# Attention scores from two fp32r parts on half the array's rows, in place of three bf16 parts on half its columns

## What is computed

```python
x = x + 0.5 * ffn(layernorm(x))
h = layernorm(x)                                  # (16, 256, 256)
q, k, v = (heads(h @ W.T) for W in (Wq, Wk, Wv))  # 16 heads of 16
q, k = rope(q), rope(k)
s = where(causal, q @ k.T / 4, -inf)              # (16, 16, 256, 256)
x = x + merge(softmax(s) @ v) @ Wo.T
x = x + 0.5 * ffn(layernorm(x))
```

## Time and profile before

| what | us |
|---|---|
| runs | 603.33 median, 602.26 to 603.72 |
| profiled execution, span from first to last instruction | 600.8 |
| median less that span | 2.5 |
| PE / PEld busy | 567.2 / 496.4 |
| DVE / ACT / POOL busy | 458.9 / 345.2 / 229.3 |

### The profile page before, as it was taken

The page is one execution under the profiler, slowest core; times in us unless marked ns, Lnnn a source line. Parts: engine busy times, 40 slices in busy tenths (PEclk is TensorE's granted clock), DMA queues, the critical chain, the costliest instruction groups (busy, mean ns, idle before and its releaser), DMA issues.

```text
span 600.8 us, 17866 instructions
## 1 busy us (share of the span) xinstructions
PE 567.2 (94%) x6596; PEld 496.4 (83%) x6596; DVE 458.9 (76%) x928; ACT 345.2 (57%) x610; POOL 229.3 (38%) x446
## 2 busy tenths in 40 slices
PE   1999999999789999999999999999888999999998
PEld 1789999999668888888888888888665788999997
DVE  5977777779797978879788788877562777777765
ACT  2765454546246666776667766567545655455453
POOL 6383333332665354444544445434141033333310
PEclk9999999999999999999999999999989999999999
DMA  6530000000987567654576546765400011111111
GB/s 221 199 112 6 0 0 0 0 0 1 257 219 207 167 164 208 172 157 146 166 204 177 158 139 175 197 186 159 138 2 3 1 36 35 35 35 35 35 35 36
DMA packets 71190, 63.45 MB, mean 106 GB/s; under 512 B 4178, under 2 KB 64370, under 8 KB 71154
## 3 DMA queue, kind: packets, MB, share of 16 engines
q1 hardware_dynamic: 69970, 62.81, 36.1%
q10 hardware_dynamic: 1184, 0.14, 0.2%
HBM read 33.03 MB, written 29.36 MB: 104 GB/s over the span
## 4 chain that ended last, share of the span: by engine, by line
PE 82%; DVE 10%; DMA 3%; ACT 2%; issue 1%; POOL 1%; SPq 1%; ACTq 0%; DVEq 0%
PE bank L173 18%; PE bank L537 18%; PE bank L1065 13%; PE bank L673 6%; PE bank L1060 6%; PE bank L1121 5%; PE bank L1196 4%; PE bank L1161 3%; PE bank L156 2%; PE bank L1124 2%; PE bank L1134 2%; DVE mx L863 2%; DVE g_lo L257 2%; PE bank L1184 1%; DMA w1f<-w1t 1%
## 5 line engine op out<-in xcount | busy, mean ns | idle before, releaser
L863 DVE TENSOR_REDUCE mx<-bank 128x2 f32<-128x512 f32 (+1 forms) x192 | 118.7, 684 | 31.3 <-PE bank L1065 31.2
L240 ACT ACTIVATE g<-bank,b1c 128x512 f32<-128x512 f32 x128 | 88.0, 690 | 65.6 <-PE bank L173 62.5
L537 PE MATMUL bank<-w2q,g_hi 128*128 128x256 f32 x512 | 124.4, 284 | 1.3 <-DVE g_lo L257 0.9
L537 PE MATMUL bank<-w2q,g_lo 128*128 128x256 f32 x512 | 122.5, 280 | 0.0
L985 ACT ACTIVATE probs<-bank 128x512 f32<-128x512 f32 x192 | 111.2, 597 | 11.9 <-PE bank L1065 4.4
L537 PEld LDWEIGHTS bank<-w2q,g_hi 128*128 128x128 f32 x512 | 96.5, 188 | 2.9 <-DVE w2q L375 1.1
L537 PEld LDWEIGHTS bank<-w2q,g_lo 128*128 128x128 f32 x512 | 96.5, 188 | 0.6
L315 POOL TENSOR_TENSOR res<-res,b2h 128x1024 f32 (+1 forms) x16 | 38.3, 2394 | 133.0 <-DVE xn L147 128.9
L257 DVE TENSOR_TENSOR g_lo<-g,g_hi 128x512 fp32r<-128x512 f32 x128 | 82.8, 689 | 3.1
L173 PE MATMUL bank<-xt_hi,w1q 128*128 128x512 f32 x240 | 77.3, 404 | 2.0 <-DVE xt_lo L167 2.0
L173 PE MATMUL bank<-xt_lo,w1q 128*128 128x512 f32 x240 | 76.4, 400 | 0.0
(11 more groups left out here) (129 smaller groups left out, 1170.1 us busy)
## 6 DMA issues: line engine op xcount, KB each, us to landing
qk_slots<-parts SPq DMA_DIRECT2D x32, 384.0 KB, 3.6
q<-qk_slots SPq DMA_DIRECT2D x32, 384.0 KB, 4.0
k<-qk_slots SPq DMA_DIRECT2D x32, 384.0 KB, 4.5
qk_slots<-parts SPq DMA_DIRECT2D x32, 256.0 KB, 3.4
res<-x SPq DMA_DIRECT2D x8, 512.0 KB, 3.6
qk_slots<-parts SPq DMA_DIRECT2D x32, 128.0 KB, 3.2
out<-res SPq DMA_DIRECT2D x7, 512.0 KB, 2.9
w1f<-w1t SPq DMA_DIRECT2D x2, 512.0 KB, 6.1
```

Of the source, the lines that this page charges most:

```text
L240: nc.scalar.activation(g[:, f, :], of[:], ACT.Gelu, bias=b1c[:, f:f + 1]).then_inc(g_ready, 1)
L537: last = nc.tensor.matmul(to[:, 0:D], part[:, f, t * P:(t + 1) * P], w2q[:, f, :], start=f == 0 and part is g_hi, stop=f == FC - 1 and par ...
L863: nc.vector.tensor_reduce(o, i, AX.X, ALU.max).then_inc(s_done, 1)
```

## The change

q and k become two fp32r parts (top and low): three products of parts, 48 rows, with 3 fence rows and 2 of the maxima 53, which fit into half the array's rows. Even batches live in partitions 0 to 63, odd ones in 64 to 127 of one tile each for q and k. `units` issues a straight product of batch p+1 and a turned one of batch p by turns, on the two row halves, over all 128 output columns; the two fence products come last, with an identity, or one with its halves swapped where input and output halves differ. The middle part, its rest on VectorE and its cast on ScalarE go (also in the turning at the end of the first feed-forward stage); the stores are four per batch, of the same bytes. xn is made by GpSimd, in two ops over two row tiles. The maxima are two fp32r parts, transposed as fp32 into a projection bank; those of half 1 are now transposed in the period after (MT(p, 1) is of batch p). att_t is allocated outside the stage and first holds the constant rows; a swapped identity is made by GpSimd in the first feed-forward stage (a memset and two selects). The period is laid out in four groups, in all engines' lists: on VectorE maxima 0, rope 0, normed 0, maxima 1, rope 1, statistics, maxima 2, normed 1, low_att, maxima 3, low_xt, add_output; on ScalarE exponentials 0, copy_heads 0, copy_max 1, exponentials 1, top 0, copy_max 0, exponentials 2, copy_heads 1, copy_v, copy_att, exponentials 3, copy_xt, top 1. In the last period ScalarE does both gelus' work ahead of copy_att. Cut to its core:

```diff
-PARTS = 3
-SLOTS = 6
+PARTS = 2
+SLOTS = 3
...
-Q_RUNS = ((0, 0, 2), (2, 0, 3), (5, 0, 1))
-K_RUNS = ((0, 0, 3), (3, 0, 1), (4, 0, 2))
+Q_RUNS = ((0, 0, 1), (1, 0, 2))
+K_RUNS = ((0, 0, 2), (2, 0, 1))
...
-        q6, k6 = zip(*([sb(f"{n}6_{p}", [ROWS, HEADS, SEQ], BF16) for n in "qk"] for p in range(2)))
+        q_rows, k_rows = (sb(f"{n}_rows", [P, HEADS, SEQ], F32R) for n in "qk")
...
+        def rows(of, par, first, end):
+            return of[HALF_ARRAY * par + first:HALF_ARRAY * par + end]
...
+                par = p.parity(1 - h)
+                sp.wait_ge(mt_sb, 2 * (p.p + 1 - h) + h + 1)
+                sp.dma_start(rows(q_rows, par, SCORED, ROWS)[:, HALF * h:HALF * h + HALF, :].bitcast(F32), mt[h][:].bitcast(F32))\
+                  .then_inc(m_loaded[par][h], 16)
...
+            def step(p):
+                if p.has(0):
+                    max_rows(p, 1)
                 if p.has(2):
-                    load(p, h)
-                if h == 1 and p.has(3):
+                    load(p, 0)
+                if p.has(3):
                     store(p, 0, Q_RUNS)
+                if p.has(1):
+                    max_rows(p, 0)
+                if p.has(2):
+                    load(p, 1)
+                if p.has(3):
...
+                pool.tensor_tensor(m_parts[:, :, 0, :].bitcast(F32R), mx[:, h, :, :], zero[:], ALU.add).then_inc(max_s, 1)
+                pool.wait_ge(max_s, 2 * n + 1)
+                pool.tensor_tensor(m_parts[:, :, 1, :].bitcast(F32R), mx[:, h, :, :], m_parts[:, :, 0, :], ALU.subtract)\
+                    .then_inc(max_s, 1)
...
+                pool.wait_ge(top_s, 2 * b + t + 1)
+                pool.tensor_tensor(parts[par][:, t, 1, :], rot[:, t, :], parts[par][:, t, 0, :].bitcast(F32), ALU.subtract)\
+                    .then_inc(low_s, 1)
...
+            def normalise(p):
+                b, par = p.p + 4, p.parity(4)
+                pool.wait_ge(rstd_s, 2 * p.turn(4))
+                if p.has(2, 2):
+                    pool.wait_ge(xt_lo_s, b - 3)
+                own = slice(QT * par, QT * par + QT)
+                pool.tensor_tensor(xn[:, own, :], res[:, bass.ts(b, QT), :], mean[:, own].unsqueeze(2).broadcast_to([P, QT, D]),
+                                   ALU.subtract).then_inc(xn_s, 1)
+                pool.wait_ge(xn_s, 2 * b - 3)
+                pool.tensor_tensor(xn[:, own, :], xn[:, own, :], rstd[:, own].unsqueeze(2).broadcast_to([P, QT, D]),
+                                   ALU.mult).then_inc(xn_s, 1)
+            def step(p):
...
+                if opening:
+                    normals(p)
+                if p.has(1):
+                    pad(p)
...
+                if p.has(3):
+                    rotate(p, 0)
+                if p.has(1):
+                    split_max(p, 0)
+                if p.has(3):
+                    low(p, 0)
+                    rotate(p, 1)
+                if p.has(4, 2):
+                    normalise(p)
+                if p.has(3):
+                    low(p, 1)
+                if p.has(1):
+                    split_max(p, 1)
+                if p.par == 1 and p.has(5, 2, BATCH - 2) and not opening:
+                    normals(p)
...
+            def exponentials(p, g):
+                for u, at in enumerate((4 * SEQ, 0, 2 * SEQ)):
+                    n = 3 * g + u
+                    if n % 6 == 0 and (p.has(-1) or g):
+                        act.wait_ge(pv_done, 2 * p.p + g // 2)
                     act.wait_ge(t_ready, UNITS * p.p + n + 1)
...
+            def fence(to, mask, par, half):
+                own = slice(HALF_ARRAY * par, HALF_ARRAY * par + HALF_ARRAY)
+                return nc.tensor.matmul(to[:, :, bass.ts(half, HALF_ARRAY)], (ident_b if half == par else ident_swap)[own, :],
+                                        mask[own, own].unsqueeze(1).broadcast_to([HALF_ARRAY, to.shape[1], HALF_ARRAY]), start=False, stop=half == 1, skip_group_check=True)
+            def score(to, weights, moving, first):
+                nc.tensor.matmul(to, weights, moving, start=first, stop=False, skip_group_check=True)
+            def units(p, n):
+                g, u = n // 3, n % 3
+                straight, turned_too = p.has(1), p.has(0)
+                if straight:
+                    b, par = p.p + 1, p.parity(1)
+                    if n == 0 and not p.has(-1):
+                        pe.wait_ge(swap_ready, 3)
+                        pe.wait_ge(rows_in[par], 48)
+                        pe.wait_ge(y_done, CT * CHUNKS + 2)
+                    if n % 6 == 0:
+                        pe.wait_ge(loaded[par][n // 6], LOADS * (p.turn(1) + 1))
+                    if p.has(0) or n >= 3:
+                        pe.wait_ge(s_done, UNITS * b + n - 2)
+                    s, s_par = s_ring[u], par
+                    q, k = rows(q_rows, par, 0, SCORED), rows(k_rows, par, 0, SCORED)
+                if turned_too:
+                    if n % 6 == 0:
+                        pe.wait_ge(m_loaded[p.par][n // 6], 16 * (p.turn(0) + 1))
+                    if p.has(-1) or n >= 2:
+                        pe.wait_ge(t_done, UNITS * p.p + n - 1)
+                    t, t_par = t_ring[n % 2], p.par
+                    tq, tk = rows(q_rows, t_par, 0, ROWS), rows(k_rows, t_par, 0, ROWS)
                 if u == 0:
-                    fence(r[:].rearrange("p (a k) -> p a k", a=4), mask_qk[:, 0:4, :])
                     for j in range(4):
-                        h = 4 * g + j
-                        last = halves(r[:, j * P:(j + 1) * P], q[0:SCORED, h, 0:P], k[0:SCORED, h, 0:P], j == 3)
+                        h, at = 4 * g + j, slice(j * P, (j + 1) * P)
+                        if straight:
+                            score(s[:, at], q[:, h, 0:P], k[:, h, 0:P], j == 0)
+                        if turned_too:
+                            score(t[:, at], tk[:, h, P:SEQ], tq[:, h, P:SEQ], j == 0)
                 else:
-                    fence(r[:].rearrange("p (a k) -> p a k", a=2)[:, :, P:SEQ], mask_qk[:, 0:2, :])
                     for j in range(2):
-                        h = 4 * g + 2 * u - 2 + j
-                        last = halves(r[:, j * SEQ:(j + 1) * SEQ], q[0:SCORED, h, P:SEQ], k[0:SCORED, h, :], j == 1)
...
+                        h, at = 4 * g + 2 * u - 2 + j, slice(j * SEQ, (j + 1) * SEQ)
+                        if straight:
+                            score(s[:, at], q[:, h, P:SEQ], k[:, h, :], j == 0)
+                        if turned_too:
+                            score(t[:, at], tk[:, h, 0:P], tq[:, h, :], j == 0)
+                for half in range(HALVES):
+                    if straight:
+                        to = s[:].rearrange("p (a k) -> p a k", a=4) if u == 0 else s[:].rearrange("p (a k) -> p a k", a=2)[:, :, P:SEQ]
+                        s_last = fence(to, mask_qk, s_par, half)
+                    if turned_too:
+                        to = t[:].rearrange("p (a q) -> p a q", a=4) if u == 0 else t[:].rearrange("p (a q) -> p a q", a=2)[:, :, 0:P]
+                        t_last = fence(to, mask_kq, t_par, half)
+                if straight:
+                    s_last.then_inc(s_ready, 1)
+                if turned_too:
+                    t_last.then_inc(t_ready, 1)
+            def group(p, g):
+                for n in range(3 * g, 3 * g + 3):
+                    units(p, n)
...
+                pe.wait_ge(max_s, 2 * (2 * (p.p + 1 - h) + h) + 2)
+                if h == 0:
+                    if p.has(3):
+                        pe.wait_ge(rope_s, 2 * (p.p + 3) + 1)
+                    elif p.has(-2):
+                        pe.wait_ge(att_lo_s, p.p - 1)
+                elif p.has(-2):
+                    pe.wait_ge(wo_done, p.p)
+                else:
+                    pe.wait_ge(v_done, p.p + 3)
                 for t in range(QT):
-                    last = nc.tensor.transpose(mt_bank[:, t * P // 2:(t + 1) * P // 2].bitcast(BF16),
...
+                group(p, 0)
...
+                if p.has(3):
+                    QK(p, 0)
+                if p.has(0):
+                    MT(p, 1)
+                if p.has(-1):
+                    OT(p, 0)
+                group(p, 1)
...
+                if p.has(3):
+                    QK(p, 1)
+                if p.has(0):
+                    PV(p, 0)
                 if p.has(1):
-                    MT(p, h)
+                    MT(p, 0)
+                group(p, 2)
...
+                if p.has(3):
+                    V(p)
+                if p.has(-1):
+                    ANT(p)
                 if p.has(0):
-                    PV(p, h)
+                    OT(p, 1)
+                group(p, 3)
+                if p.has(4, 2):
+                    XT(p)
...
+                if p.has(-1):
+                    WO(p)
...
+                if p.has(0):
+                    PV(p, 1)
```

463 lines of the change are left out of this document (172 added, 291 removed).

## The result

The changed kernel takes **641.0 us** (median of 4 runs, 637.72 to 641.99) against 603.13 (602.26 to 603.72) in the same session: ratio 1.0611, interval 1.0591 to 1.063. The forecast was 617 with a range up to 638: right in sign, about 24 us short. The profiled execution's span is 638.7 us against 600.8, so 37.9 us are to be found.

What follows compares the result with a forecast made beforehand. TensorE's program of a period was taken as the bound: +1.0 us a period gave +13, the start +2.4, the last two periods -1.5, so 13.9 on a 600.8 us span; forecast 617 us, range 594 to 638.

Steps and rivals of the forecast that it cites:

- What bounds the kernel: In an attention period, TensorE's own program sets the length, 18.76 us; the change was priced as its new length.
- the two-bank wait: In each group, the third step waits for the first exponential to free its turned bank: half a microsecond.
- C: In scoring, loads on the two row halves queue for one path: 2.55 us a group, 646 us; chance 0.10.
- A: In scoring, loads cost 0.055 us and tiling overheads hide: groups of 1.73 us, 596 us; chance 0.16.
- B: In scoring, row halves give all they can: 1.1 us a group, 570 us; chance 0.06.
- the exit: On TensorE, the time from the last score pairs to the transposes behind them, 0.10 us each.
- A group's length: In scoring, three steps take 2.00 us with the wait, four groups 8.0; scoring +0.6 us a period.
- step 1: The second of a group's three steps, load-bound at 0.33 us and over at 1.04 us.
- Changes of tiling: On TensorE, eleven a period in place of six, each 0.10 us: +0.5 us a period (0 to 0.9).
- The last two periods: At the end of attention, without projections, the new order should leave fewer waits: -1.5 us (-3 to 0).
- The opening: At the stage's start, xn made on GpSimd delays XT and scoring: +2.4 us (0 to 5).
- Work off TensorE: On VectorE, ScalarE, GpSimd and stores, the changed work is all covered by TensorE's period.

Runs made afterwards that it cites:

- The other order: The changed kernel with the long unit (four heads) second instead of first in each group, on all engines: 622.76 us, ratio 1.0335.
- the short exponential: The changed kernel with the first exponential of each group reading 64 of its 512 columns, ones in place of the rest: 614.69 us, ratio 1.0164.
- bursts of two and the earlier copy: The changed kernel with six bursts of two units, normalisation on VectorE, and low_att ahead of the second half of the heads' normalisation: 606.6 us, ratio 1.0051.
- all three kernels of the table: The changed kernel (641.0 us), the same with the long unit second (622.76 us), and the same with a shortened first exponential (614.69 us).

## Why the prediction was right and wrong

**What bounds the kernel** held: the time is TensorE's program of a period, with the two-bank wait in it, and the forecast named that wait, its place and its cause. The other order and the short exponential show it. The forecast was short by 24 us all the same: four terms of its sum failed, and they are the first four points below the table.

**Rivals.** C, loads that queue, was ruled out by the first rows of a group: the turned product starts with the straight one. A, cheap loads, is ruled out by the repeat of 0.11 to 0.12 us where it needs 0.055, and its groups of 1.73 by 2.17. B supposed that the row halves give all they can, and in this it was right. The Trainium skill, TensorEngine Tiling (Array Packing), section Theoretical Speedup, puts that at up to 2x for such contractions. The trace agrees: a second set of 14 matmuls on the other half adds 0.02 us to 1.61. B failed on its price of 1.1 us a group, which is that of the columns (1.07): with loads of 0.11 us, fences and the exit the group takes 1.63, and the exponential, which B needed not to be last, makes it 2.17.

**The sizes, by stretch**, with the clock's third taken out (1.3 us of before, 6.9 and 2.5 of after):

| stretch | forecast | measured |
|---|---|---|
| opening, to the fourth projection to v | +2.4 and half a period's 1.0 = +2.9 | +1.7 |
| twelve periods | +12.0 | +21.4 |
| last stretch | -1.5 and half a period's 1.0 = -1.0 | +6.8 |
| clock | 0 | +8.0 |
| sum | +13.9 | +37.9 |

- *A group's length* is the first step that failed. Forecast 2.00 and 0.10 for the exit; measured 2.17 in one period and up to 2.27 in the next: 8.84 on average for four against 8.40. The parts were all low, by 0.02 to 0.12 us. Without the wait I had 1.58 (step 1 over at 1.04, then 0.44 and the exit), measured 1.63; the wait I had at 0.52, it is 0.54 and in three groups of every second period 0.64. An error of 5% in a group costs nearly 6 us over 13 periods.
- *Changes of tiling* and the rest of the period: forecast 11.4, measured 11.66, another 0.3 us a period. The unit price of 0.1 was right. Each stage of twelve projection matmuls behind a group takes 1.54 against half of the 2.95 that both took in one piece, 0.07 more; an exposed first load would be 0.11, and the forecast had that as its upper bound only. That it is the load isn't shown.
- *The last two periods* have the wrong sign: -1.5 in the forecast. I expected fewer waits; there are more. Without projections the stages between groups are short, and copies and exponentials on ScalarE get no cover. On TensorE's timeline of the changed kernel:

```profile
452.79 0.66 PE L1138 MATMUL bank<-ident,o_sb 128*128 128x128 f32 x4 [0.80 <-ACT o_sb L974]
455.08 0.35 PE L1061 MATMUL bank<-k_rows,q_rows 51*128 51x256 f32 x1 [0.44 <-DVE mx L877]
456.40 0.64 PE L1125 MATMUL bank<-probs,v_pad 128*32 128x256 f32 x8 [0.69 <-ACT probs L982]
```

  The middle row is the two-bank wait again: the maximum that it names isn't what this step waits for. The short exponential brings the stretch from 74.08 (2.5 of it the clock's) to 66.88, bursts of two and the earlier copy to 66.00, which is the kernel before's 66.13.
- *The granted clock* was not in the forecast at all, which put it at nothing without a reason; with the changed kernel's low stretches it is a fifth of the loss. The four runs of the changed kernel go with it: 637.72 us at a mean clock of 0.984, 640.46 at 0.979, 641.53 and 641.99 at 0.976.
- *The opening*: the term of 2.4 for the late start measured 2.7, with the cause as forecast.
- *Every second period* is 0.28 us longer (20.64), with the third step 0.1 later in three of its groups. This is part of the wait: it is there in all three kernels of the table on the third step, and in the kernel of 606.6, where no burst has a third step, bursts of 1.20, 1.25 and 0.98 us are as long in either period. Straight and turned change halves with the period's parity; why the release then takes 0.14 in place of 0.05 is open.

*Work off TensorE* was costed at nothing, rightly: in the list of TensorE's waits nothing in a full period waits for GpSimd or a transfer.

## What to carry to other kernels

When a two-deep ring already stops the pipeline once, shortening the producer's work buys only a longer wait there. Price the loop (the producer's issue, the latency, the reader, the release) first, and move other work into it before making the products cheaper. Breaking twelve units into bursts no longer than the ring, with independent stages between, won back 26 of 38 us here with no product changed, and the next wait that this uncovered was worth another 6.5. A run that shortens a wait doesn't show what is left without it: compare the start of the step with the end of what it waited for. The idle time in a row, which counts from modelled ends, gave 0.35 us for a wait of 0.54, and nothing for one of 0.17.

## What the runs showed of the hardware

Loads and matmuls of fp32r on 51 to 53 rows of the two row halves start within 0.01 us of each other and repeat every 0.10 to 0.12 us (320.44, 320.56, 320.66), as loads on all rows do. With both halves busy a group's own work takes 1.63 us, with one 1.61. They run side by side even when all products of one half are issued ahead of the other's: a turned product started ahead of a straight one that stands before it in the program (237.55 and 237.76). With four products and two fences ahead of it it came 0.28 us late, and this order cost 3.2% in all. A third step started 0.05 or 0.14 us behind the end of the exponential that freed its bank, depending on the period's parity. The low granted clock of 0.5 cost a third of its duration and moved between the opening and the end of attention when only the opening was changed; the runs of one variant spread over 1.3 to 8.9 us, those of the kernel before over 1.5 to 3.1.
